# Attention in units of two source tiles, the ones multiplied with every weighed tile

## The reference, cut to what matters

```python
q = k = h @ qk_w.T + qk_b            # one matrix for both
v = h @ v_w.T + v_b
score[e] = clip(dot(k[src[e]], q[dst[e]]) / 8, -5, 5)
w[e] = exp(score[e])
out[n] = sum(w[e] * v[src[e]] for e into n) / sum(w[e] for e into n)
```

## Time and profile before

| | us |
|---|---|
| median of 3 runs | 7713.19 |
| lowest, highest | 7692.12, 7717.1 |
| span of the profiled execution | 5940.5 |
| attention in it, first score to last write | 4654.3 to 5399.4 |

### The profile page before, as it was taken

One profiled execution on the slowest core, in us unless ns is written; L12 is line 12 of the kernel. 1 busy time (PEld: TensorE's weight loads), 2 busy tenths in 40 slices (PEclk: granted clock), 3 DMA queues, 4 the chain that ended last, 5 costly groups with the idle time before them and its releaser, 6 DMA issues. The chain is left out here.

```text
span 5940.5 us, 172794 instructions
## 1 busy us (share of the span) xinstructions
PE 5149.6 (87%) x40520; PEld 3768.8 (63%) x40521; DVE 4123.0 (69%) x13309; ACT 2673.9 (45%) x5408; POOL 3052.2 (51%) x3157
## 2 busy tenths in 40 slices
PE   2889989989899857988888899898687899995999
PEld 2667767666676645666666666666586433334989
DVE  7777777777777776777777777777723788886232
ACT  1444444444444434444444444444311688884010
POOL 4577777777777737777777777777200000000000
PEclk9999999999999989999999999999898999997999
DMA  3444444444444425444444444444184233332969
GB/s 86 106 105 112 112 108 100 109 110 110 109 111 100 109 54 124 102 108 110 109 109 110 109 99 112 110 109 109 32 346 184 93 115 110 114 110 76 381 271 355
DMA packets 695806, 764.66 MB, mean 129 GB/s; under 512 B 369203, under 2 KB 618138, under 8 KB 670625
## 3 DMA queue, kind: packets, MB, share of 16 engines
q1 hardware_dynamic: 568261, 577.66, 31.7%
q0 software_dynamic: 100352, 102.96, 9.0%
q10 hardware_dynamic: 27102, 82.91, 3.9%
HBM read 671.04 MB, written 88.81 MB: 128 GB/s over the span
## 5 line engine op out<-in xcount | busy, mean ns | idle before, releaser
L336 POOL DMA_INDIRECT gat_rows<-rows_scr,gat_idx x3136 | 3025.7, 965 | 1093.7 <-issue 895.5
L1172 ACT ACTIVATE adj_tiles<-gat_counts 128x392 f32 (+1 forms) x784 | 389.9, 497 | 1570.5 <-PE gat_counts L1258 1533.6
L1022 DVE TENSOR_SCALAR adj_hot_key<-adj_iota_key,adj_winbase,adj_key 128x392 bf16<-128x392 int16 x2416 | 951.3, 394 | 0.3 <-issue 0.3
L1308 PE MATMUL gat_sps<-gat_relu,gat_att 128*128 128x256 f32 x3136 | 860.5, 397 | 0.0
L1071 DVE CUSTOM_DVE_ANT_0 gat_masked<-gat_sps,gat_miss,gat_oldtop 128x512 f32<-128x512 f32 x784 | 588.4, 751 | 311.1 <-PE gat_sps L1308 309.9
L1299 PE MATMUL gat_aps<-gat_rows,gat_weightsT 128*128 128x65 f32 x6224 | 793.5, 271 | 0.0
L1299 PEld LDWEIGHTS gat_aps<-gat_rows,gat_weightsT 128*128 128x128 f32 x6224 | 769.2, 195 | 0.0
L1021 DVE TENSOR_SCALAR adj_hot_lo<-adj_iota_lo,adj_low 128x128 bf16<-128x128 int16 x2416 | 658.2, 272 | 156.4 <-PE gat_counts L1245 79.0
L1275 PE MATMUL gat_mps<-gat_ea,gat_we 128*128 128x256 f32 x1568 | 493.2, 396 | 259.9 <-issue 157.9
L1290 PE MATMUL gat_tps<-ident,gat_weights 128*128 128x128 f32 x3136 | 520.8, 289 | 159.2 <-ACTq L1155 138.1
L1151 ACT ACTIVATE gat_weights<-gat_masked,gat_newtop 128x512 f32<-128x512 f32 x788 | 562.4, 714 | 67.4 <-DVE gat_newtop L1071 36.3
(11 more groups left out here) (372 smaller groups left out, 6678.5 us busy)
## 6 DMA issues: line engine op xcount, KB each, us to landing
gcn_sum_adj<-adj_scr SPq DMA_DIRECT2D x98, 1568.0 KB, 8.4
gat_dstb<-dst_scr SPq DMA_DIRECT2D x784, 128.0 KB
gat_ea<-in_ea SPq DMA_DIRECT2D x784, 128.0 KB
gin_sum_adj<-adj_scr SPq DMA_DIRECT2D x49, 1568.0 KB, 8.5
adj_scr<-adj_tiles ACTq DMA_DIRECT2D x48, 1568.0 KB
at_adj<-adj_scr SPq DMA_DIRECT2D x84, 896.0 KB, 5.0
gat_rows<-rows_scr,gat_idx POOLq DMA_INDIRECT x3136
gat_xr<-xr_scr SPq DMA_DIRECT2D x1568, 24.0 KB
```

The costliest lines, as they stand in the source:

```text
L336: pool.indirect_dma_start(ring.rows[:, u, c, 0:ROW], None, rows_d, bass.IndirectOffsetOnAxis(ap=ring.idx[:, u, c:c + 1], axis=0)).then_inc ...
L1022: dve.tensor_scalar(plan.hot_key[:, slot, :], plan.iota_key[:], plan.winbase[:, bass.ds(w, 1)], plan.key[:, bass.ds(c, 1)], ALU.add, ALU.i ...
L1308: last = pe.matmul(sps[j][:, h * (GE // 2):(h + 1) * (GE // 2)], att[:, h, :], relu[:, j, :], start=True, stop=True)
```

## The change

Everything goes in *units* of two source tiles (24 units and tile 48). A score bank pair of 1024 columns holds a unit, there are two of them; `ex` and the weights hold units too, 4 and 6 of them, laid out with the two tiles interleaved by target tile so that one VectorE instruction matches the adjacency's layout. `low`, `late`, `direct`, `clip` and `weigh` each work on 1024 columns. Even units go through `low` and `late`, odd units through `direct` and `clip`. `join` and its buffer are gone; the ones are multiplied with every weight tile, once for every two units, right after the second one's values. `vps` is doubled. Tile 48's score goes to the bank of `fps`. The last group, one target tile wide, takes eight source tiles as a unit (6 units and tile 48). Adjacency has a buffer for a whole group, loaded in 6 pieces of 8 tiles (the last 9), a piece as soon as its tiles of the group before are weighed.

```diff
+    ES, WS = 4, 6
+    LAG = 4
...
+        adj = k.sb("at_adj", [P, GT, NT * P], BF16, own)
+        ex = k.sb("at_ex", [P, ES, GT, 2, P], F32, own)
+        ex_end = k.sb("at_ex_end", [P, W], F32, own)
+        wt = k.sb("at_wt", [P, WS, GT, 2, P], F32, own)
+        wt_end = k.sb("at_wt_end", [P, W], F32, own)
+        sums = k.sb("at_sums", [P, W], F32, own)
...
+        sps = [k.ps(f"at_s{j}", [P, U], F32, own) for j in range(2)]
+        vps = [k.ps(f"at_v{j}", [P, W], F32, own) for j in range(2)]
+        dps = k.ps("at_d", [P, W], F32, own)
...
+        def blocks(u, tiles):
+
+            if tiles == GT:
+                return [(2 * u + h, h, slice(0, GT)) for h in range(2)]
+            return [(2 * GT * u + 2 * q + h, h, slice(q, q + 1)) for q in range(GT) for h in range(2)]
+
+        def turned_unit(bank):
+
+            return bank[:].rearrange("p (h a d) -> p a h d", h=2, d=P)
+
+        def flat(unit):
+            return unit.rearrange("p a h d -> p (a h d)")
+
...
+                    sp.wait_ge(s_weight, units_of(g, (4 * p + 3 if p < NPC - 1 else UNITS) - (UNITS + 1)))
+                    at = slice(p * PIECE * P, ((p + 1) * PIECE if p < NPC - 1 else NT) * P)
+                    sp.dma_start(adj[:, 0:tiles, at], adj_d[bass.ds(g * GT, tiles), :, at].rearrange("a p f -> p a f")
+                                 ).then_inc(s_in[p], 16)
+
+            def ask_next(g, slot, tiles=GT):
+                sp.wait_ge(s_score, units_of(g - 2, UNITS))
...
+            def score(g, u, tiles, odd):
+                if u == UNITS:
+                    if tiles == GT:
+                        pe.wait_ge(s_out, g + 1)
+                    pe.matmul(end_score(tiles), keys[0:D, END, :], ask[0:D, odd, 0:tiles, :].rearrange("p a n -> p (a n)"),
+                              start=True, stop=True).then_inc(s_score, 1)
+                    return
+                if u < 2:
+                    if u == 0:
+                        pe.wait_ge(s_low, lows_of(g, UNITS - 2 - UNITS))
                     else:
-                        pe.wait_ge(s_low, lows_of(g, c - Q))
-                    rows = slice(c % 2 * D, c % 2 * D + D)
-                    pe.matmul(sps[c % 4][:, 0:tiles * P], keys[rows, c, :],
-                              ask[rows, odd, 0:tiles, :].rearrange("p a n -> p (a n)"),
-                              start=True, stop=True).then_inc(s_score, 1)
-
...
+                for c, h, at in blocks(u, tiles):
+                    rows = slice(h * D, h * D + D)
+                    last = pe.matmul(sps[u % 2][:, h * W + at.start * P:h * W + at.stop * P], keys[rows, c, :], ask[rows, odd, 0:tiles, :].rearrange("p a n -> p (a n)"),
+                                     start=True, stop=True)
+                last.then_inc(s_score, 1)
...
+            def value(g, u, tiles, odd):
                 w = tiles * P
-                if j == 0:
+                if u == 0:
                     pe.wait_ge(s_evac, g + 1)
-                pe.wait_ge(s_weight, weights_of(g, z - 1))
-                if j == NQD - 1:
...
-                if j % 2 == 1:
-                    pe.wait_ge(s_sum, sums_of(g, z // 2 - 1))
-                    for h in range(4):
-                        last = pe.matmul(dps[32 * h:32 * h + 32, 0:w], ones[:, 0:32], two[:, (j // 2 % 2) * 4 + h, 0:w],
-                                         start=(j == 1), stop=False)
-                last.then_inc(s_quad, 1)
...
+                else:
+                    for c, h, at in blocks(u, tiles):
+                        last = pe.matmul(vps[odd][h * D:h * D + D, 0:w], values[:, c, :], wt[:, u % WS, at, h, :],
+                                         start=(c < 2), stop=False)
+                last.then_inc(s_value, 1)
+
+            def total(g, jj, tiles):
+                w = tiles * P
+                if jj == 0:
+                    pe.wait_ge(s_evac, g + 2)
+                for n, (c, h, at) in enumerate(blocks(2 * jj, tiles) + blocks(2 * jj + 1, tiles)):
+                    u = 2 * jj + (n >= len(blocks(0, tiles)))
+                    last = pe.matmul(dps[32 * (n % 4):32 * (n % 4) + 32, 0:w], ones[:, 0:32], wt[:, u % WS, at, h, :],
+                                     start=(jj == 0 and n < 4), stop=False)
+                last.then_inc(s_ones, 1)
+
...
+                n = units_in(tiles)
+                for u in range(n):
+                    score(g, u, tiles, odd)
+                    if u >= LAG:
+                        value(g, u - LAG, tiles, odd)
+                        if (u - LAG) % 2 == 1:
+                            total(g, (u - LAG) // 2, tiles)
                     elif not first:
-                        total(g - 1, NQD - 2 + j, GT)
-                    if j == 3 and not first:
+                        value(g - 1, u + UNITS + 1 - LAG, GT, 1 - odd)
+                        if u % 2 == 0:
+                            total(g - 1, UNITS // 2 - 2 + u // 2, GT)
+                        if u == LAG - 1:
+                            total_end(GT)
+                    if u == (9 if tiles == GT else n - 1) and not first:
                         turn_back(g - 1, GT)
+                score(g, UNITS, tiles, odd)
+                if tiles == GT:
+                    value(g, UNITS - LAG, tiles, odd)
...
+            def direct(g, u):
+                act.wait_ge(s_score, units_of(g, u))
+                act.wait_ge(s_weight, back(g, u, ES))
+                act.activation(ex[:, u % ES, :, :, :], turned_unit(sps[u % 2]), ACT.Exp, scale=1.0 / 8.0).then_inc(s_exp, 1)
...
+            def low(g, u):
+                act.wait_ge(s_score, units_of(g, u))
+                act.wait_ge(s_weight, back(g, u, ES))
+                act.activation(ex[:, u % ES, :, :, :], turned_unit(sps[u % 2]), ACT.Relu, bias=five[:], scale=1.0 / 8.0).then_inc(s_low, 1)
+
+            def late(g, u):
+                act.wait_ge(s_low, lows_of(g, u))
+                act.activation(flat(ex[:, u % ES]), flat(ex[:, u % ES]), ACT.Exp, bias=minus[:]).then_inc(s_late, 1)
+
+            def group(g, odd, first=False):
+                for u in range(0, UNITS, 2):
+                    low(g, u)
+                    direct(g, u + 1)
+                    late(g, u)
+                    if u == 2 and not first:
+                        evacuate(g - 1, GT, 1 - odd)
+                direct_end(g, GT)
...
+            def clip(g, u):
+                e = flat(ex[:, u % ES])
+                dve.wait_ge(s_exp, directs_of(g, u))
                 dve.tensor_scalar(e, e, HIGH, LOW, ALU.min, ALU.max).then_inc(s_clip, 1)
...
+                dve.wait_ge(s_in[piece], g * 16 + 16)
+                dve.wait_ge(s_value, back(g, u, WS))
+                dve.wait_ge(s_ones, ones_of(g, (u - WS) // 2) if u >= WS else ones_of(g - 1, (u + UNITS - WS) // 2))
+                if is_direct(u):
+                    dve.wait_ge(s_clip, directs_of(g, u) - AHEAD)
                     dve.tensor_tensor(w, e, a, ALU.mult).then_inc(s_weight, 1)
                 else:
-                    dve.wait_ge(s_late, lows_of(g, c) - FREE)
+                    dve.wait_ge(s_late, lows_of(g, u) - AHEAD)
                     dve.scalar_tensor_tensor(w, e, HIGH, a, ALU.min, ALU.mult).then_inc(s_weight, 1)
 
-            def join(g, c, w):
-                dve.wait_ge(s_weight, weights_of(g, c + 1))
-                dve.tensor_tensor(two[:, c // 2 % 8, 0:w], wt[:, wt_slot(c), 0:w], wt[:, wt_slot(c + 1), 0:w], ALU.add
-                                  ).then_inc(s_sum, 1)
...
+            def group(g, first=False):
+                for u in range(0, UNITS, 2):
+                    clip(g, u + 1)
+                    weigh(g, u, GT)
+                    weigh(g, u + 1, GT)
+                    if u == 14 and not first:
                         finish(g - 1, GT)
-                clip(g, END, tiles * P)
-                join(g, END - 2, tiles * P)
```

More of the change, by code:

```diff
@@ L1844, in attention @@
     LAST = NT - GROUPS * GT
[L1845 to L1850, removed]
-    END = NT - 1
+    W = GT * P
+    U = 2 * W
+    END = NT - 1
+    UNITS = END // 2
+    FEW = END // (2 * GT)
+    PIECE = 8
+    NPC = END // PIECE
+    ES, WS = 4, 6
+    LAG = 4
     AHEAD = 64
-    PAIRS = NT // 2
-    LOWS = END // Q * (Q - 1)
     LOW, HIGH = float(np.exp(-5.0)), float(np.exp(5.0))
     s_set, s_ask = k.sem("at_set"), [k.sem(f"at_ask{j}") for j in range(2)]
[L1858 to L1861, removed]
+    s_in = [k.sem(f"at_in{j}") for j in range(NPC)]
+    s_low, s_late, s_ones = (k.sem("at_" + n) for n in ("low", "late", "ones"))
+    s_score, s_exp, s_clip, s_weight, s_value, s_evac, s_fold, s_out = (
+        k.sem("at_" + n) for n in ("score", "exp", "clipped", "weight", "value", "evac", "folded", "out"))
     with ExitStack() as own:
@@ L1937, in _ @@
         def _(pe):
[L1938 removed]
+            pe.sem_inc(s_score, AHEAD)
+            pe.sem_inc(s_value, AHEAD)
+            pe.sem_inc(s_ones, AHEAD)
             pe.wait_ge(s_set, 1)
```

(48 more changed lines are left out.)

175 lines of the change are left out of this document (72 added, 103 removed).

## The result

| | before | after |
|---|---|---|
| median of the runs, us | 7712.44 | 7786.76 |
| lowest, highest | 7692.12, 7717.1 | 7776.28, 7811.67 |
| ratio, 95% interval | | 1.0083 [1.0048, 1.0118] |
| span of the profiled execution | 5940.5 | 7777.4 |
| attention, first score to last write | 745.1 | 807.3 |

The changed kernel is slower by 74 us. The profiled execution of before was not like the runs timed beside it: in it the part ahead of attention, nearly all of it the two GAT stages, ran some 1800 us faster (a second profile of the same kernel, e1, has a span of 7743.9). The period of attention is the same in both, 59.47 and 59.46; its last group is not (see e1).

The account below looks back on a forecast made before the run. Attention was taken as bound by TensorE: 2.9 at the start, 11 x 5.98 for the groups and -6.3 at the end gave +62.4 us. Added to 7713.2 this forecast 7776 us, with an 8-in-10 range of 7738 to 7825.

Parts of the forecast that it names:

- The bound: Full attention group: TensorE's own work sets the period, 65.5 us after the change against 59.47 before.
- The ones: TensorE, full group: ones with all 48 tiles, 12 blocks of four instead of 6, +6.0 us.
- The blocks: TensorE, full group: twice as many, shorter score and value blocks cost 2.4 and 1.8 us more.
- Rival C: Between TensorE blocks: the block's own cost goes and the kernel is faster, 7659 us; chance 0.05.
- The waits: TensorE, full group: 4.1 of the old 59.47 us are waits, which the new order loses.
- rival B: Attention groups: TensorE's waits of 4.1 us a group stay, 45 us more, 7821 us; chance 0.10.
- Start +2.9 and end -6.3: First and last attention groups: group 0 from 58.4 to 61.3 us, the last from 32.5 to 26.2.
- The sum +62.4: Whole attention: 2.9 at the start, 11 groups at 5.98 more, less 6.3 at the end, in us.
- VectorE 37.5 and ScalarE 41 at most: Full attention group: work of these engines in us, below TensorE's 65.5.
- rival D: Values and ones reading interleaved weights: strided reads at half rate, about 8120 us; chance 0.05.
- The 1772.7 us: Outside attention: gap between the profiled span, 5940.5, and the median, 7713.2, taken as unchanged.
- The landing of a 1 MB piece of adjacency: Adjacency loads: 4.7 to 5.0 us for 0.9 MB, wanted by VectorE about 7.7 us later, no cost.

Follow-up runs that it names:

- e8: The changed kernel with one useless 1024-wide VectorE addition for every pair of units: period 65.46 us, attention 807.3 us.
- e4: The changed kernel without every second block of ones: period 59.48 us, 5.98 less; attention 735.6 us.
- e5: The changed kernel with TensorE's order alone changed to two units' scores, two units' values, then ones: period 61.10 us; whole kernel 1.0005 of before.
- e2: The kernel before without joins, ones multiplied with every weight tile: period 62.95 us, attention 785.9 us.
- e3: The kernel before with TensorE's order alone changed to blocks of two scores and two values: period 63.72 us in the mean, 61.94 at full clock.
- e6: e5 with 1024-wide joins back on VectorE and ones on their sums: 5882.21 us against 5955.6 for before, ratio 0.9885; period 55.12 us.
- e7: e6 with six second-level sums a group on GpSimd and ones on sums of eight tiles: 6013.05 us, ratio 1.0099; period 65.42 us in the mean.

## Why the prediction was right

By its steps:

- The bound. TensorE's own work as the period was the claim; the period is 65.46 where the sum of block prices said 65.5, with nothing idle between 6500 and 7200, and e8 shows from the other side that VectorE's share is worth nothing.
- The ones, +6.0 a group: e4 takes half of them out and gets 5.98 back.
- The blocks, +4.2: e5 gets 4.36 back, 0.3 of it from blocks at the group's end that it merges besides. Rival C, that a block's own cost would go, is dead: ones follow their values with no wait between and pay the same. The Trainium skill's "TensorEngine Tiling (Array Packing)", under Key Properties, says that a change of tiling mode drains the engine. The traces agree that every such change costs, 0.14 to 0.20 us a block (1.06, 1.01 and 1.00 for two steps that inside a block take 0.86), and in e5 two steps without a change of mode cost nothing: four scores over two pairs of banks take 1.92, and the values of a unit and of tile 48 take 1.44 in one block, where two blocks would take 1.59.
- The waits, -4.1: gone to the last. The prediction didn't split their cause. e2 and e3 do in part: 1.7 of the 4.1 lie around the evacuation of the one bank of values, and that wait stays without the joins and is 2.8 us with short blocks; the other 2.4 go with the joins. In the new loop they are gone even with VectorE 92% full (e6), so rival B is dead for this order; which of its differences does it is open.
- Start +2.9 and end -6.3: measured +2.7 (61.1 for 58.4) and -6.3 (26.2 for 32.5). The sum +62.4 stands against +62.2. That agreement holds for the profile that the sum was read from. Against e1 the end is -10.2 and attention +58.3, because the old kernel's last group ran in part at the lower clock there.
- VectorE 37.5 and ScalarE 41 at most: measured 38.35 and 39.53; the durations from the slope between two widths, 1215 and 1150 ns, came out at 1218 and 1141; the clip's 0.69, chosen between two bounds, at 0.694.
- Strided reads (rival D): no cost, a block of two values takes 1.01, as it does in e3, where the reads are not strided.

So the 6.0 us a group are 6.0 + 4.2 - 4.1: a gain of the new loop hidden under two costs, one larger than it and one of its size.

Three things in it were wrong and didn't decide. The 1772.7 us between the profile's span and the median were taken as a constant of the kernel; they are no time outside the span, the first profiled execution was simply another kind of execution, and in every later one the span is about 2 us below its own time (7777.4 for 7779.88). It nearly cancelled, since all of attention but the last group ran alike in both. The landing of a 1 MB piece of adjacency was taken as 5 us; several pieces are now asked for at once and the tile's view gives

```profile
DMA to landing us min/median/max: 5.2/10.4/14.3
```

which is 10.4 in the median, and still nobody waited for it. And the measured total, +74, is 12 us over the sum, or 16 over the 58.3 that attention gives against e1, whose kind the timed runs were. That the forecast, 7776, lies within 11 us of the measured 7786.76 is in part luck, then. What scatters is the part ahead of attention: in the executions e1 to e4 and the changed kernel's first one, whose code up to attention is one and the same, attention starts between 6428.5 and 6513.5 us. Whether a part of the difference belongs to the change stays open; the profiles show no place for it.

## What to carry to other kernels

Price TensorE by distances from start to start of whole blocks, and count blocks as well as products: where work alternates between different shapes of the array, every block pays for its opening and its end (0.14 to 0.20 us here), so group the same shape as far as the PSUM banks allow. Taking work off an engine that waits for another is worth only the waits that the other has left; in the new loop 13 us of additions on VectorE cost nothing (e8), while the ones on TensorE that replaced them cost 6. A change that loses can hold a part that gains: e6 keeps the new loop, undoes the two costs and is 4.35 us a group faster than before. And look at the granted clock before a difference is called a wait: in e3 half of the periods are 2.9 us longer by the clock alone.

## What the runs showed of the hardware that was not expected

- The same program took near 5950 us in some executions and near 7750 in others, on one and the same chip; the difference lies ahead of attention, in the main in the two GAT stages, where the granted clock was 0.98 in one and 0.84 in the other over the same window. The periods of attention, in which TensorE is busy 58.9 of 59.5 us, ran at 1.00 and agree to 0.01 us; its last group ran at 1.00 in one (32.5 us) and at 0.86 in the other (36.3 us). Why was not tested.
- A short wait of TensorE can cost more than its length. In e3 a wait of 2.75 us stands at each group's start; in seven of ten periods the granted clock fell to 0.5 for 3.4 or 6.8 us about when it ended, and the period grew from 61.94 to 63.6 or 64.8. In before, with 0.54 us idle at that place, it stayed at 1.00 in every full period.
- An elementwise addition of 128x1024 float32 on GpSimd took 2.3 to 14 us beside a busy VectorE (e7; the profile's times of GpSimd are rough), and VectorE's clips stretched by 56% (690 ns in e6 to 1074) and single additions from 1.2 to 3.4 us.
